# Second attention in another order: output product in the last but one unit's bank, scores, sums and weighing moved

## The reference, cut to what matters

```python
def _L1_xattn_ref(query, key_value, Wq, bq, Wk, bk, Wv, bv, Wo, bo):
    ...
    Q = (query @ Wq.T + bq).reshape(B, SQ, H, Dh).transpose(0, 2, 1, 3)
    K = (key_value @ Wk.T + bk).reshape(B, SKV, H, Dh).transpose(0, 2, 1, 3)
    V = (key_value @ Wv.T + bv).reshape(B, SKV, H, Dh).transpose(0, 2, 1, 3)
    scale = jnp.asarray(np.sqrt(Dh), query.dtype)
    scores = jnp.einsum('bhqd,bhkd->bhqk', Q, K) / scale
    weights = jax.nn.softmax(scores, axis=-1)
    attn = jnp.einsum('bhqk,bhkd->bhqd', weights, V)
    attn = attn.transpose(0, 2, 1, 3).reshape(B, SQ, H * Dh)
    return attn @ Wo.T + bo
...
x = x + _L0_xattn_ref(_layernorm(x), ctx_1024, ctx_1024, ...)
x = x + _L0_ffn_ref(_layernorm(x), ...)
x = x + _L1_xattn_ref(_layernorm(x), ctx_1024, ...)
x = x + _L1_ffn_ref(_layernorm(x), ...)
```

## Time and profile before

| | |
|---|---|
| median of 3 runs | 744.39 us (744.32 to 747.69) |
| profiled execution | 746.67 us |
| its span | 744.9 us |
| busy share: PE, PEld, DVE, ACT, POOL | 93%, 77%, 67%, 45%, 40% |
| second attention, steps 0 to 15 | about 397 to 592 us |
| mean DMA rate over the span | 109 GB/s |

### The profile page before, as it was taken

How to read it: one execution, slowest core, us unless ns; L and a number is a source line. 1 busy time by engine, 2 the same in 40 slices (tenths; PEclk the granted TensorE clock), 3 DMA queues, 4 the chain that set the end, 5 groups by cost and what they waited for, 6 DMA issues and landing times.

```text
span 744.9 us, 16708 instructions
## 1 busy us (share of the span) xinstructions
PE 695.1 (93%) x6469; PEld 577.0 (77%) x6469; DVE 501.1 (67%) x1262; ACT 337.6 (45%) x691; POOL 294.8 (40%) x224
## 2 busy tenths in 40 slices
PE   5899999989999999999998999999988899999998
PEld 4678788865578899888785676666766787899998
DVE  4788888887862244301667878788888767767465
ACT  2122222237844122212766777778787452332323
POOL 2333333428851333323435778787868000000000
PEclk9999999999999999999998999999999999999999
DMA  9979000006867956541463887777670000000000
GB/s 287 358 237 53 26 26 26 26 25 172 208 154 155 249 163 211 167 138 19 107 150 71 152 168 163 163 163 140 149 143 3 2 1 14 1 26 1 26 13 27
DMA packets 65611, 81.55 MB, mean 109 GB/s; under 512 B 32018, under 2 KB 55154, under 8 KB 64226
## 3 DMA queue, kind: packets, MB, share of 16 engines
q1 hardware_dynamic: 62434, 72.68, 41.4%
q0 software_dynamic: 2816, 3.67, 2.6%
q10 hardware_dynamic: 288, 4.19, 1.3%
HBM read 60.45 MB, written 19.31 MB: 107 GB/s over the span
## 4 chain that ended last, share of the span: by engine, by line
PE 65%; DVE 18%; DMA 6%; issue 4%; ACT 4%; POOL 2%; SPq 0%; DVEq 0%; POOLq 0%; ACTq 0%
PE psum L1192 7%; PE psum L1177 7%; PE psum L855 6%; PE psum L2461 6%; DVE mx L1956 5%; PE psum L2160 5%; PE psum L1623 5%; DMA kparts_d<-kp 4%; PE psum L345 3%; PE psum L2121 3%; DVE rsum L1979 3%; PE psum L2183 2%; PE psum L887 2%; PE psum L1631 2%; PE psum L1644 2%
## 5 line engine op out<-in xcount | busy, mean ns | idle before, releaser
L1956 DVE TENSOR_REDUCE mx<-psum 112x2 f32<-112x750 f32 x128 | 113.5, 926 | 13.6 <-PE psum L2121 13.0
L1863 ACT ACTIVATE probs<-psum 125x448 f32<-125x448 f32 x192 | 91.1, 545 | 27.3 <-PE psum L2147 27.2
L855 PE MATMUL psum<-w_parts,c_parts 128*125 128x512 f32 x288 | 74.8, 412 | 9.6 <-DVE w_parts L623 7.9
L1761 POOL TENSOR_TENSOR half_sum<-probs 125x896 f32<-125x896 f32 x30 | 62.7, 2090 | 37.4 <-ACT probs L1863 37.4
L855 PEld LDWEIGHTS psum<-w_parts,c_parts 128*125 128x125 f32 x288 | 54.1, 192 | 24.0 <-DVE w_parts L623 7.9
L2121 PE MATMUL psum<-kpk,qpk 96*128 96x375 bf16 x256 | 61.5, 332 | 8.9 <-DVE mx L1956 8.8
L2147 PEld LDWEIGHTS psum<-qpk,kpk 128*128 128x128 bf16 x768 | 47.5, 100 | 25.7 <-issue 12.5
L2147 PE MATMUL psum<-qpk,kpk 128*128 128x112 bf16 x768 | 61.7, 217 | 5.3 <-ACT probs L1863 3.5
L1767 POOL TENSOR_TENSOR tile_sum<-half_sum,probs 125x896 f32<-125x896 f32 x30 | 62.5, 2085 | 2.4
L1465 ACT ACTIVATE ctx_all<-psum,cols 128x448 f32<-128x448 f32 (+1 forms) x40 | 22.4, 561 | 82.2 <-PE psum L1631 82.2
L1033 ACT ACTIVATE hT<-psum,b 128x224 f32<-128x224 f32 x64 | 25.2, 444 | 73.4 <-PE psum L1177 73.4
(11 more groups left out here) (237 smaller groups left out, 1479.9 us busy)
## 6 DMA issues: line engine op xcount, KB each, us to landing
we<-in_we SPq DMA_DIRECT2D x6, 2048.0 KB, 8.6
kparts_d<-kp SPq DMA_DIRECT2D x16, 562.5 KB, 5.3
kpk<-kparts_d SPq DMA_DIRECT2D x16, 562.5 KB, 6.3
ctx_all<-in_ctxT SPq DMA_DIRECT2D x16, 375.0 KB, 3.9
kpk<-kparts_d SPq DMA_DIRECT2D x16, 375.0 KB, 7.2
we<-in_we ACTq DMA_DIRECT2D x2, 2048.0 KB, 15.6
kpk<-kparts_d SPq DMA_DIRECT2D x16, 187.5 KB, 4.0
qparts_d<-qp SPq DMA_DIRECT2D x16, 168.0 KB, 3.5
```

The lines of the kernel that those rows point to most:

```text
L855: ins = pe.matmul(banks[B_KV[t]][0:KT, :], parts_of[:, x, k, t * KT:(t + 1) * KT], w_parts[:, k, w], start=(k == 0 and (x, w) == SPLIT[0]) ...
L1761: pool.tensor_tensor(half_sum[:, m], probs[:, m, 0], probs[:, m, 1], ALU.add)\
L1863: act.activation(probs[:, m, t, g * HU * SQ:(g + 1) * HU * SQ], banks[B_ST[u % 3]][0:KT, 0:HU * SQ], ACT.Exp, scale=SCALE)\
L1956: dve.tensor_reduce(mx[:, n % 2, H + 2 * j:H + 2 * j + 2], psum[0:SQ, first:first + 2, 0:SK], AX.X, ALU.max)\
```

## The change

It reorders the sixteen steps and takes one operation out of them.

- `out_product` is written into bank 5 (all 256 columns in one bank) instead of the banks 0 and 1, and stands behind S7. It waits for the exponential of unit 10, the last unit in bank 5. Unit 1 of the next step waits for the residual, which reads that bank. In the last step the product of entry 14 keeps its banks and its place.
- `weigh(n, 0)` moves from behind S7 to between S5 and S6, which both stand behind unit 9. S3 moves up by one unit, S4 and S5 back by one.
- S0 of entry n+2 moves ahead of `shift_turn`, and `add_up(n, 0)` ahead of `weigh(n, 1)`.
- `shift_turn` becomes a transpose of 112x128 on the whole array, twice, where it was two matmuls on 32 columns; for that the maxima lie at the columns 112 to 127 of a wider `mx`.
- `add_bias` goes. The bias of the values times the output weights is added to the output bias once, by two matmuls and one addition in the expert stage.
- On DVE `normalise` moves behind maximum 3 (in the last step it keeps its place). On ACT `zero_padded` moves from behind exponential 11 to behind exponential 8.

On PE a step then reads: u0, add_up(n-1, 1), u1, u2, S2, u3, S3, u4 to u7, S4, u8, u9, S5, weigh(n, 0), S6, u10, u11, S7, out_product(n-1), S0 of n+2, shift_turn(n+1), S1 of n+2, add_up(n, 0), weigh(n, 1).

The hunks left out below move three small tensors to other places in SBUF and add or remove semaphores.

```diff
--- before.py
+++ after.py
@@ -48,6 +48,7 @@
 ROWS = TERMS * HD
 SHIFT = 2
 TURNED = SHIFT * H
+MAX_AT = 128 - H
 Q_HIGH, Q_LOW = NR - 1, 0
 AHEAD = 3
 VW = NKT * D
@@ -59,8 +60,9 @@
 
 
 FIRST_SCORES = {4: (0, 1), 5: (2, 3, 4), 6: (5, 6, 7)}
-SCORES_AFTER, OUT_AT = {2: 2, 4: 3, 6: 4, 8: 5, 9: 6}, 6
-INVERT_AT, NORM_AT = 2, 3
+SCORES_AFTER, WEIGH_AFTER = {2: (2,), 3: (3,), 7: (4,), 9: (5, 6), 11: (7,)}, 5
+PAD_AFTER = 8
+INVERT_AT, NORM_AT, TEAM_AT = 2, 4, 3
 VALUES_AFTER = {0: (B - 3, B - 2), 1: (B - 1,)}
 STATS_AHEAD = 5
 WEIGHT_PARTS = 4 + 4 + 2 + 3
...
@@ -1127,6 +1130,8 @@
 
         for s in range(2):
             find(0, s)
+        dve.tensor_tensor(rows1[0:SQ, 0:D], rows1[0:SQ, 0:D], banks[B_IDX][0:SQ, 128:128 + D], ALU.add)\
+            .then_inc(out_bias_done.sem, 1)
         for s in range(2):
             keep(0, s, True)
             find(1, s)
@@ -1194,6 +1199,9 @@
                                     start=(f == 0), stop=(f == FC - 1))
             ins.then_inc(fc2_ps.sem, 1)
 
+        for m in range(KC):
+            pe.matmul(banks[B_IDX][0:SQ, 128:128 + D], bv1[:, m:m + 1].broadcast_to([128, SQ]), wo1[:, m],
+                            start=(m == 0), stop=(m == KC - 1))
         pe.wait_ge(parts_done.sem, 4)
         find(0, 0)
         value(pe, 3, range(NKT), 0)
...
@@ -1290,15 +1300,12 @@
     tile_sum = sb(ctx, "tile_sum", [KT, KC, HC * SQ])
     half_sum = sb(ctx, "half_sum", [KT, KC, HC * SQ])
     probs = sb(ctx, "probs", [KT, KC, NKT, HC * SQ])
-    mx = sb(ctx, "mx", [SQ, 2, 3 * H])
+    mx = sb(ctx, "mx", [SQ, 2, 128 + H])
     high = sb(ctx, "high", [128, SQ], BF16)
     shift = sb(ctx, "shift", [128, SQ], BF16)
-    lower = sb(ctx, "lower", [128, 1])
-    own = sb(ctx, "own", [128, H], BF16)
     first_exp = sb(ctx, "first_exp", [1, 1])
     rsum = sb(ctx, "rsum", [128, KC, SQ])
     au = sb(ctx, "au", [128, KC, SQ])
-    aT1 = sb(ctx, "aT1", [128, KC, SQ])
     xb1 = sb(ctx, "xb1", [SQ, 2, D])
 
     w_in = sem(root, "w_in", 16)
...
@@ -1374,7 +1380,15 @@
     pv = banks[B_PV][:, 0:KC * SQ].rearrange("p (m q) -> p m q", m=KC)
     sums = banks[B_PV][:, KC * SQ:2 * KC * SQ].rearrange("p (m q) -> p m q", m=KC)
     turned = banks[B_ST[0]][ROWS:, 0:SQ]
-    product_of = lambda n: psum[0:SQ, (B_S[0] if n + 1 < B else 5):(B_S[0] if n + 1 < B else 5) + 2, 384:512]
+    B_PRODUCT = 5
+    LAST_IN_PRODUCT = max(u for u in range(UNITS) if B_ST[u % 3] == B_PRODUCT)
+
+    def product_of(n):
+
+        if n + 2 < B:
+            return banks[B_PRODUCT][0:SQ, 0:D].rearrange("p (m c) -> p m c", m=KC)
+        first = B_S[0] if n + 1 < B else B_PRODUCT
+        return psum[0:SQ, first:first + 2, 384:512]
 
     B_T, B_Y = 4, 6
     CHUNKS = 4
@@ -1751,6 +1765,8 @@
 
             if b >= 2:
                 pool.wait_ge(x3_done.sem, x3_done.at(b - 2))
+            elif b == 0:
+                pool.wait_ge(out_bias_done.sem, out_bias_done.at(0))
             pool.tensor_tensor(xb1[:, b % 2], x_all[:, b], rows1[0:SQ, 0:D], ALU.add).then_inc(xb1_done.sem, 1)
 
         def add_tiles(n):
@@ -1844,15 +1860,6 @@
                 act.activation(qpk[ROWS:, n % AHEAD, heads], spread(shift[ROWS:], 1, count), ACT.Copy)\
                     .then_inc(spread_done.sem, 1)
 
-        def add_bias(n):
-
-            act.wait_ge(au_done.sem, au_done.at(n))
-            if n:
-                act.wait_ge(wo1_ps.sem, wo1_ps.at(n - 1))
-            for m in range(KC):
-                ins = act.activation(aT1[:, m], au[:, m], ACT.Identity, bias=bv1[:, m:m + 1])
-            ins.then_inc(aT1_done.sem, 1)
-
         def step(n):
             for u in range(UNITS):
                 m, t, g = unit(u)
@@ -1863,8 +1870,8 @@
                 act.activation(probs[:, m, t, g * HU * SQ:(g + 1) * HU * SQ],
                                banks[B_ST[u % 3]][0:KT, 0:HU * SQ], ACT.Exp, scale=SCALE)\
                     .then_inc(exp1_done.sem, 1)
-                if u == 5 and n:
-                    add_bias(n - 1)
+                if u == PAD_AFTER and n + 1 < B:
+                    zero_padded(n + 1)
                 if u == 2 and n >= SPLIT_FROM:
                     if n == SPLIT_FROM:
                         act.wait_ge(w_in.sem, w_in.at(WEIGHT_PARTS, 0))
@@ -1880,7 +1887,6 @@
                     if u == 6:
                         gate_exp(act, 0)
             if n + 1 < B:
-                zero_padded(n + 1)
                 spread_shift(n + 1)
 
         spread_shift(0)
@@ -1889,7 +1895,6 @@
             step(n)
         relu(act, 0, 0)
         relu(act, 0, 1)
-        add_bias(B - 1)
         relu(act, 0, 2)
         relu(act, 0, 3)
 
@@ -1953,7 +1958,7 @@
             if j == 0 and n == 0:
                 dve.wait_ge(lower_done.sem, lower_done.at(1))
             first = B_S[j % 2]
-            dve.tensor_reduce(mx[:, n % 2, H + 2 * j:H + 2 * j + 2], psum[0:SQ, first:first + 2, 0:SK], AX.X, ALU.max)\
+            dve.tensor_reduce(mx[:, n % 2, MAX_AT + 2 * j:MAX_AT + 2 * j + 2], psum[0:SQ, first:first + 2, 0:SK], AX.X, ALU.max)\
                 .then_inc(max_done.sem, 1)
 
         def shifts(n):
@@ -1980,7 +1985,7 @@
 
         def normalise(n):
             if n:
-                dve.wait_ge(aT1_done.sem, aT1_done.at(n - 1))
+                dve.wait_ge(wo1_ps.sem, wo1_ps.at(n - 1))
             dve.wait_ge(rsum_done.sem, rsum_done.at(n))
             dve.wait_ge(pv_ps.sem, pv_ps.at(n))
             dve.tensor_tensor(au[:], pv, rsum[:], ALU.mult).then_inc(au_done.sem, 1)
@@ -2032,11 +2037,11 @@
                     team_ahead(n)
                 if j == INVERT_AT and n:
                     invert_sums(n - 1)
-                if j == NORM_AT and n:
+                if j == (NORM_AT if more else TEAM_AT) and n:
                     normalise(n - 1)
                 if more:
                     two_max(n + 1, j)
-                if j == NORM_AT and not more:
+                if j == TEAM_AT and not more:
                     team_entry()
             if n and more:
                 add_x(n - 1)
@@ -2127,8 +2132,8 @@
             if n:
                 pe.wait_ge(exp1_done.sem, exp1_done.at(n - 1, UNITS - 2))
             for r in range(SHIFT):
-                ins = pe.matmul(turned, mx[:, n % 2, (1 - r) * H:(3 - r) * H], ident[0:SQ, 0:SQ], start=(r == 0),
-                                stop=(r == SHIFT - 1), tile_position=(0, ROWS))
+                ins = pe.matmul(banks[B_ST[0]][:, 0:SQ], mx[:, n % 2, (1 - r) * H:(1 - r) * H + 128],
+                                ident[0:SQ, 0:SQ], start=(r == 0), stop=(r == SHIFT - 1), is_transpose=True)
             ins.then_inc(turn_ps.sem, 1)
 
         def transposed_scores(n, u):
@@ -2141,6 +2146,8 @@
                 pe.wait_ge(exp1_done.sem, exp1_done.at(n, u - 2))
             elif n and u == 0:
                 pe.wait_ge(exp1_done.sem, exp1_done.at(n - 1))
+            elif n >= 2 and u == 1:
+                pe.wait_ge(x3_done.sem, x3_done.at(n - 2))
             for c in range(HU):
                 h = m * HC + g * HU + c
                 at = h * SK + t * KT
@@ -2177,10 +2184,12 @@
                 ins.then_inc(sums_ps.sem, 1)
 
         def out_product(n):
-            pe.wait_ge(aT1_done.sem, aT1_done.at(n))
+            pe.wait_ge(au_done.sem, au_done.at(n))
+            if n + 2 < B:
+                pe.wait_ge(exp1_done.sem, exp1_done.at(n + 1, LAST_IN_PRODUCT + 1))
             for half in range(2):
                 for m in range(KC):
-                    ins = pe.matmul(product_of(n)[:, half], aT1[:, m], wo1[:, m, half * 128:(half + 1) * 128],
+                    ins = pe.matmul(product_of(n)[:, half], au[:, m], wo1[:, m, half * 128:(half + 1) * 128],
                                     start=(m == 0), stop=(m == KC - 1))
             ins.then_inc(wo1_ps.sem, 1)
 
@@ -2198,27 +2207,24 @@
                     out_product(n - 1)
                 if u == 9 and not more:
                     bias_product()
-                j = SCORES_AFTER.get(u)
-                if j == OUT_AT and n and more:
-                    pe.wait_ge(max_done.sem, max_done.at(n + 1, OUT_AT - 1))
-                    out_product(n - 1)
-                if j and more:
-                    score(n + 1, j)
-            if more:
-                score(n + 1, H // 2 - 1)
-            weigh(n, 0)
-            if more:
-                shift_turn(n + 1)
-            if n + 2 < B:
-                if n:
-                    pe.wait_ge(x3_done.sem, x3_done.at(n - 1))
-                for j in range(2):
-                    score(n + 2, j)
+                for j in SCORES_AFTER.get(u, ()):
+                    if more:
+                        score(n + 1, j)
+                    if j == WEIGH_AFTER:
+                        weigh(n, 0)
             if not more:
                 marked(pe, 0)
+                weigh(n, 1)
+                return
+            if n:
+                out_product(n - 1)
+            if n + 2 < B:
+                score(n + 2, 0)
+            shift_turn(n + 1)
```

(5 more changed lines are left out.)

6 lines of the change are left out of this document (4 added, 2 removed).

## The result

On one chip, 20 runs each, the kernel after took 743.12 us in the median against 747.18 before. The ratio over all these runs is 0.9951, with a 95% interval of 0.9936 to 0.9967. That is 3.7 us less (747.18 x 0.0049; the two medians lie 4.1 apart), where 10.7 had been forecast. Two more comparisons of the same kernel gave 0.9971 (0.9943 to 0.9999) and 0.9962 (0.9931 to 0.9993).

The account below looks back on a forecast made before the run. The attention step was taken as a loop of waits with no engine full. Gains 7.9 + 0.3 + 0.6 + 1.0 + 1.1 - 0.2 = 10.7 us, taken from the median 744.39, gave 733.7; range from half a microsecond below 731 to 739.5.

Parts of the forecast that it names:

- (a): Second attention's steps: output product behind S7, first weighing between S5 and S6, normalising after M3; walked step 10.8 us.
- my walk: Ordinary attention step followed through DVE's and PE's work with old durations, without POOL or keys: 10.8 us.
- POOL's loop: Attention step: POOL's four additions, second sums, then the next step's first half-sum: a loop of 10.92 us.
- my last rival: Change doesn't do what it says: product's new wait makes DVE wait; step 11.6, whole 740 to 742; chance 0.07.
- (b): Bias add removed from ACT: worth nothing in ordinary steps; in the last step PE had waited 1.29 us for it.
- (c): Turn of the maxima as real transpose: 0.22 us instead of 0.44, priced from four expert-stage transposes at 0.11 each.
- (d): Formerly covered loops, POOL 10.92 and keys 11.1 at median landing: step 11.76 to 11.1, twelve steps less 7.9 us.
- keys later: Rival: denser traffic raises key landings to 7.5 or 7.7, step 11.4 to 11.6, whole 737 to 740; chance 0.2.
- (e): End steps: first less 0.3 us, two weight-splitting steps less 0.6 and 1.0, last step less 1.1 of 1.29.
- (f): Value bias folded into output bias at the expert stage's start: plus 0.2 us, bounds 0 and 0.5.
- Slower: Rival: late keys before S0 hold PE longer, paying beyond 7.9 us of landing; at 8.4, 747.6; chance 0.04.

Follow-up runs that it names:

- experiment 7: Kernel after with all weights of the last part loaded in step 11 of the program: ratio 1.0013, twelve steps 132.3 us; a second single run, 134.9 us.

## Why the prediction was right and wrong, step by step

**(a) The reordered loop: right in size, wrong in what closes it.** 10.97, against 10.8 from my walk, 10.92 from POOL's loop and 11.1 with keys. That it came within 0.1 of POOL's number is partly luck, since another loop sets it. The two maxima did go beside PE's work. But the loop isn't the one that I walked (reciprocal, maxima, product, PE), nor POOL's. The chain of a clean step shows ACT at its corners: start us, us, what.

```profile
446.54 1.43 ACT probs L1870 x3
...
452.05 0.55 ACT probs L1870
...
452.74 1.10 PE psum L2192 x8
453.83 0.32 PE psum L2126 x2
454.16 0.21 PE psum L2135 x2
...
454.39 0.27 ACT high L1856
...
454.68 0.35 DVE shift L1969
...
455.53 1.40 ACT qpk L1860 x2
456.93 0.02 issue
456.95 0.54 ACT probs L1870
```

The product's new wait for the exponential of u10, at which I looked only as 0.2 of delay, ties exponential, product, S0, turn, high part, shift, three copies and the next exponentials into one ring: exponentials 1.43, PE's units, scores and first weighing 3.92 up to u10 (448.10 to 452.02, left out here), its exponential 0.55, product, S0 and turn 1.63, and 3.10 from the high part to the end of the next first exponential (454.39 to 457.49); with 0.34 between them 10.97. It is the mechanism of my last rival at a lower price. I had excluded it by ACT's busy time, 9.16 of 11.73; busy time doesn't tell whether an engine's waits lie inside a ring. The half columns of POOL settled that it isn't POOL's. The ring itself is read from the chain; no run took the product's wait out of it.

**(b) The bias add** cost nothing in the steps, as said: with the fold alone they stay 11.73. **(c) The turn** takes 0.21 on the chain as two records, 0.22 forecast. The Trainium skill, TensorE: Matmul & The Clock Gate, section Terms, has the transpose mode four times faster for FP32. By that it would have been 0.11, an estimate (0.44 by four); the measurement differs and decides, and it is what the row of the expert stage gave.

**(d) The keys: the step that failed.** The step of the forecast that failed is its term for the keys, which gave the twelve steps 7.9. It took the median landing, 7.2, as one number for all steps, and put its loop at 11.1, a little above POOL's. The median even stayed, at 7.0. What it missed is threefold. First, the landing varied, 6.6 to 8.7, and only the late ones cost, so the mean of the cost isn't the cost of the mean; with the weights late (experiment 7) the landings that the trace shows singly were 6.4 to 7.3 until those were issued. Second, PE's own instructions are moved by the same DMA engines, in blocks of 16 KB that took 0.9 to 1.7 us each, 19 of them in the twelve steps. I put them at nothing and never looked for them in the trace: the old loop had hidden them. Third, the stall of 1.48 for keys was paid twice, by 1.7 of half clock behind it; that happened in one step of one of the three profiles. I had priced the same traffic as one rival (keys later, 0.2) at 737 to 740 without the other two terms. Twelve steps: 7.9 forecast, 2.7 in the profile (4.0 and 2.6 in the other two), with 8.8 in reach (141.1 - 132.3). The runs without keys show that all of the difference goes with the traffic; those with moved weights, that from step 3 on it takes the weights on top of the keys.

**(e) The ends.** The two split steps were to give 1.6 and gave nothing from reciprocal to reciprocal (12.70 and 12.72 for 12.61 and 12.83); from first exponential to first exponential they gave 0.1 and 0.2. ACT's two copies that split weights, 0.63 and 0.40, stood where ACT had time before; now they stand among the exponentials of the ring that ACT closes (read from the timeline below, not tried by a run of its own):

```profile
551.86 0.63 ACT L1428 ACTIVATE wi_first<-ctx_all 128x512 fp32r<-128x512 f32 x1
552.40 0.40 ACT L1428 ACTIVATE lb_parts<-ctx_all 128x256 fp32r<-128x256 f32 x1
552.70 2.69 ACT L1870 ACTIVATE probs<-psum 125x448 f32<-125x448 f32 x6
```

POOL holds these steps too: with its first additions halved, and no keys, they were 12.40 and 11.63, 0.3 and 1.1 shorter. The last step gave 0.76 (16.67 to 15.91, both at a granted clock of 1.00) of the 1.1; the 1.29 before its product is gone. From the first key issue to the first reciprocal, which holds the first step and everything ahead of it, it is 0.55 less in this pair of profiles (180.79 for 181.34), where I had 0.3 for the first step. But the other two profiles of the kernel after have 181.64 and 182.04 there, so no gain is shown.

**(f) The fold** cost 0.3 to 0.4 of PE (4.39 for 4.08; the first key issue comes 14.90 after the lookup list for 14.51), within 0 to 0.5, and not 0.2.

**The sum.** In this pair of profiles: twelve steps 2.7, the three last 0.8, the stretch up to the first reciprocal 0.5, less 0.4 for the fold: 3.6. The rest of the span's 4.1 is in stretches that the change doesn't touch and that vary by as much. That 3.6 is so near the 3.7 of the runs is luck: the 0.5 isn't reproduced, and with the lower clock in the last step the three last took 45.0 instead of 41.3.

**Slower** had its point at 7.9 us of landing. A landing of 8.7 came, but in one step of twelve.
